# Rows of maxima inside the scores' operands, and maxima set out by a table, in the two 14-wide layers of a four-layer vision network

## What is computed

```python
q, k, v = (xw @ qkv_w + qkv_b) split into 12 heads of 16
attn = q * 16 ** -0.5 @ k.T
attn = attn + rel_h[..., :, None] + rel_w[..., None, :]   # products of q with two small tables
attn = softmax(attn)            # the largest score of each query is subtracted before exp
out = attn @ v                  # then a projection, a residual sum, a norm and an MLP
```

## Time and profile before

| what | value |
|---|---|
| time, median of 3 runs | 605.55 us (603.67 to 606.29) |
| the profiled execution | 607.03 us, of which its span 605.2 us |
| busy, share of the span | PE 88%, PE weight loads 63%, DVE 49%, ACT 38%, POOL 23% |
| mean granted TensorE clock | 0.952 of 2.4 GHz |

### The profile page before, as it was taken

One profiled execution on the slowest core, in us unless ns is written; L12 is line 12 of the kernel. 1 busy time (PEld: TensorE's weight loads), 2 busy tenths in 40 slices (PEclk: granted clock), 3 DMA queues, 4 the chain that ended last, 5 costly groups with the idle time before them and its releaser, 6 DMA issues.

```text
span 605.2 us, 10070 instructions
## 1 busy us (share of the span) xinstructions
PE 530.5 (88%) x3840; PEld 382.5 (63%) x3840; DVE 296.9 (49%) x776; ACT 229.4 (38%) x453; POOL 139.7 (23%) x206
## 2 busy tenths in 40 slices
PE   6968889899988958878888999979879897999997
PEld 4726768674764545455666694756467675848676
DVE  4735866563143552655757452136566755711142
ACT  4304544535335116254544405333235446250210
POOL 8003000103005055073472216020030101120030
PEclk9979998899998979999989999989989898999999
DMA  6893547003312635616637205502916420020001
GB/s 169 190 196 72 118 103 254 1 3 96 94 58 59 134 96 134 155 47 145 145 89 173 114 1 127 123 20 57 192 43 144 92 92 2 2 67 0 1 0 53
DMA packets 21863, 55.39 MB, mean 92 GB/s; under 512 B 4560, under 2 KB 10248, under 8 KB 21688
## 3 DMA queue, kind: packets, MB, share of 16 engines
q1 hardware_dynamic: 21432, 54.65, 37.4%
q0 software_dynamic: 384, 0.10, 0.1%
HBM read 12.28 MB, written 0.79 MB: 22 GB/s over the span
## 4 chain that ended last, share of the span: by engine, by line
PE 62%; DVE 16%; SPq 8%; ACT 5%; DMA 5%; issue 4%; DVEq 0%; ACTq 0%
PE PS L1267 59%; DVE NM L1163 5%; DVE REL L1148 3%; DMA QA<-REL 2%; PE PS L1283 2%; SPq L745 2%; SPq L737 2%; ACT REL L992 2%; SPq L755 1%; DMA PT<-in_qm 1%; SPq L693 1%; ACT OT L953 1%; ACT KD L953 1%; DVE OT L1195 1%; DVE HL L1173 1%
## 5 line engine op out<-in xcount | busy, mean ns | idle before, releaser
L1163 DVE TENSOR_REDUCE NM<-PS 98x2 f32<-98x392 f32 (+2 forms) x192 | 105.7, 569 | 87.4 <-PE PS L1267 86.1
L1012 ACT ACTIVATE PT<-PS 98x392 f32<-98x392 f32 (+2 forms) x192 | 95.5, 518 | 79.0 <-PE PS L1267 77.7
L1267 PE MATMUL PS<-KA,QA 128*98 128x196 f32 (+3 forms) x432 | 90.9, 306 | 27.7 <-DVE NM L1163 22.5
L1267 PE MATMUL PS<-QA,KA 128*98 128x196 f32 (+2 forms) x480 | 91.9, 295 | 10.5 <-ACT PT L1012 5.7
L1267 PEld LDWEIGHTS PS<-KA,QA 128*98 128x98 f32 (+3 forms) x432 | 65.0, 189 | 54.6 <-DVE NM L1163 30.1
L1267 PEld LDWEIGHTS PS<-QA,KA 128*98 128x98 f32 (+2 forms) x480 | 72.9, 191 | 22.6 <-issue 12.4
L1267 PE MATMUL PS<-NR,SEL 128*98 128x392 f32 x144 | 54.4, 378 | 0.6 <-DVE NR L1185 0.6
L1267 PE MATMUL PS<-XT,WQKV 128*128 128x512 f32 (+3 forms) x104 | 49.0, 734 | 6.4 <-issue 3.3
L1267 PE MATMUL PS<-XT,W 128*128 128x512 f32 (+1 forms) x144 | 51.6, 614 | 0.0
L1267 PEld LDWEIGHTS PS<-W,HT 128*128 128x128 f32 x288 | 46.6, 190 | 4.5 <-ACT HT L1033 2.3
L1148 DVE TENSOR_TENSOR REL<-PS,REL 32x512 fp32r<-32x512 f32 (+5 forms) x64 | 28.5, 480 | 42.7 <-ACT REL L992 42.3
(11 more groups left out here) (108 smaller groups left out, 703.0 us busy)
## 6 DMA issues: line engine op xcount, KB each, us to landing
QA<-QHL SPq DMA_DIRECT2D x36, 192.0 KB
KA<-KHL SPq DMA_DIRECT2D x24, 228.0 KB
QA<-REL SPq DMA_DIRECT2D x24, 224.0 KB
QA<-QHL SPq DMA_DIRECT2D x12, 384.0 KB
KA<-KHL SPq DMA_DIRECT2D x12, 384.0 KB
KA<-PT SPq DMA_DIRECT2D x12, 380.0 KB
QA<-REL SPq DMA_DIRECT2D x24, 128.0 KB
W<-in_w SPq DMA_DIRECT2D x3, 768.0 KB, 4.4
```

The lines of the kernel that those rows point to most:

```text
L1012: nc.scalar.activation(dst, src, ACT.Exp).then_inc(probs_done.sem, 1)
L1163: nc.vector.tensor_reduce(dst, src, AX.X, ALU.max, negate=True).then_inc(max_done.sem, 1)
L1267: return nc.tensor.matmul(dst, lhsT, rhs, start=start, stop=stop, skip_group_check=loose)
```

## The change

In the 14-wide layers the maxima become ten rows of the scores' operand. KA has ten constant rows (for each part, high and low, and each of four images and the edges: one where the key belongs to it); QA has ten rows that are zero while the maxima are taken, and hold the negated maxima when the scores are. So the third matmul of each group goes, with `SEL`, `HOT` and the load of `HOT`. The ten rows are filled by another way: the transposed maxima are copied to `NR` by ACT and not by DVE, and then POOL copies them into QA, once in 784 and once in 240 columns. `scores` of a head waits for that (`rows_placed`). Slots of heads 6 to 11 hold an earlier head's maxima, so POOL zeroes the ten rows in the step `aug`, after the earlier head's scores, and the first `max` of the head waits for it (`rows_zeroed`). All other rows move to other places of the slot, with the same DMAs.

Second, the maxima are set out by a table: `add` keeps a running time of PE and DVE by fixed prices in us, and `fill` puts further `max` steps after each step while the reduction before last is finished by that account, up to three heads ahead. Third, the low parts of the second chunk's relative positions become steps of their own (`low`), two steps later, and the split of its k on POOL stands after the fourth maximum of the loop.

```diff
+        if self.pads:
+            self.max_parts = 2 * (NB + 1)
+            self.mask_row, self.rel_row = self.max_parts, 24
+            self.qk_row = self.rel_row + 2 * parts * window
...
+    for part in range(2):
+        for b in range(NB + 1):
+            masks[part * (NB + 1) + b, inner_keys(b) if b < NB else slice(FIRST_EDGE, n)] = 1
...
+PE_SHARE = {"scores": 0.20, "max": 0.18, "maxT": 0.22, "pv": 0.65, "q": 1.4, "k": 1.4, "rh": 0.5, "rw": 0.9}
+DVE_SHARE = {"max": 0.58, "parts": 0.44, "split": 2.6, "rh": 0.6, "rw": 0.6, "inverse": 1.75}
...
+    def add(step):
+        nonlocal now, busy_until
+        out.append(step)
+        if step[0] == "max":
+            now = max(now, reduced[-2])
+        now += PE_SHARE.get(step[0], 0.0)
+        busy_until = max(busy_until, now) + DVE_SHARE.get(step[0], 0.0)
+        if step[0] == "max":
+            reduced.append(busy_until)
+            if step[2] == L.max_units - 1:
+                busy_until += DVE_SHARE["parts"]
...
+    def fill(h, k):
+        needed = L.max_units * (h - 1) + 6 + k
+        while taken < len(maxima) and (taken < needed or
+                                       reduced[-2] <= now and maxima[taken][1] <= h + 3):
+            next_maximum()
...
+            elif step == "aug" and L.pads and i >= L.ring:
+                pool.wait_ge(*scores_psum.at(n, L.units * (i - L.ring + 1) - 1))
+                nc.gpsimd.memset(m["QA"][0:L.max_parts, 0, i % L.ring, :].bitcast(F32), 0.0)\
+                    .then_inc(rows_zeroed.sem, 1)
+            elif step == "maxT" and L.pads:
+                rows, src = m["QA"][0:L.max_parts, 0, i % L.ring, :], m["NR"][:, i % 2, :].bitcast(F32)
+                inner = src.rearrange("r (p q) -> r p q", p=2)[:, :, 0:HALF_IN]
+                pool.wait_ge(*maxT_done.at(n, i))
+                nc.gpsimd.tensor_copy(rows[:, 0:FIRST_EDGE].rearrange("r (b p q) -> r b p q", b=NB, p=2),
+                                      inner.unsqueeze(1).broadcast_to([L.max_parts, NB, 2, HALF_IN]))
+                nc.gpsimd.tensor_copy(rows[:, FIRST_EDGE:], src).then_inc(rows_placed.sem, 1)
...
+            elif step == "maxT" and L.pads:
+                act.wait_ge(*maxT_psum.at(n, i))
+                if i >= 2:
+                    act.wait_ge(*rows_placed.at(n, i - 2))
+                nc.scalar.activation(m["NR"][:, i % 2, :], PS[0:L.max_parts, TR_BANK, 0:2 * L.max_rows],
+                                     ACT.Copy).then_inc(maxT_done.sem, 1)
...
+                    if L.pads and h >= L.ring:
+                        pe.wait_ge(*rows_zeroed.at(n, h - L.ring))
...
-                if k == 0 and not L.pads:
-                    pe.wait_ge(*max_row_at(L, h))
+                if k == 0:
+                    pe.wait_ge(*(rows_placed.at(n, h) if L.pads else max_row_at(L, h)))
...
-                    rows = m["NR"][:, h % 2, :]
...
-                    last = mm(PS[0:size, bank, 0:wide], SEL[:, min(k, NB)].unsqueeze(1).broadcast_to([128, size]),
-                              rows, False, True, True)
```

More of the change, by code:

```diff
@@ L275, in windowed_attention, with next_maximum @@
     maxima = [("max", m, k, 0) for m in range(ahead, HEADS) for k in range(L.max_units)]
-    taken, turned, late = 0, ahead - 1, []
+    taken, turned, now, busy_until = 0, ahead - 1, 0.0, 0.0
+    reduced = [0.0, 0.0]
+    def add(step):
[9 more added lines that the diff above has]
+                busy_until += DVE_SHARE["parts"]
+    def next_maximum():
+        nonlocal taken, turned
+        add(maxima[taken])
+        taken += 1
+        if taken == 4:
+            out.append(("split", 1, 1, 0))
+        while turned < HEADS and turned < ahead + (taken - 2) // L.max_units:
+            add(("maxT", turned, 0, 0))
+            turned += 1
+    def fill(h, k):
[3 more added lines that the diff above has]
+            next_maximum()
     for h in range(HEADS):
@@ L279, in windowed_attention @@
         values = [("pv", first, k, 0) for k in range(L.pv_steps)] if h and h % L.pv_heads == 0 else []
-        goal = min(len(maxima), h * L.max_units + 5)
-        share = goal - taken
+        late = []
+        if h and (h - 1) % L.per_group == 0 and h > L.per_group:
+            g = h // L.per_group - 1
+            late = [(1, ("inverse", g, 0, 0)), (3, ("inverse", g, 1, 0)), (5, ("divide", g, 0, 0))]
+        if taken == len(maxima) and turned < HEADS:
+            add(("maxT", turned, 0, 0))
+            turned += 1
         for k in range(L.units):
-            out.append(("scores", h, k, 0))
+            add(("scores", h, k, 0))
             if h < 2 and k in (1, 4):
                 j = 4 + 2 * h + k // 4
-                out.append((*later[j], O_BANK[j % 2]))
+                add((*later[j], O_BANK[j % 2]))
+            if h < 2 and k in (3, 5):
+                j = 4 + 2 * h + k // 5
+                add(("low", later[j][0], later[j][2], O_BANK[j % 2]))
             if (h, k) == (1, 0):
-                out.append(("split", 1, 0, 0))
+                add(("split", 1, 0, 0))
             if h == 2 and k in (1, 3):
-                out.append(("aug", L.ring + k // 2, 0, 0))
+                add(("aug", L.ring + k // 2, 0, 0))
             if h >= 2 and k == L.units - 1 and h + L.ring < HEADS:
[L293 to L303, removed]
+                add(("aug", h + L.ring, 0, 0))
+            for step in values[k:k + 1] if k < NB else values[NB:] if k == NB else []:
+                add(step)
+                fill(h, k)
+            for at, step in late:
+                if at == k:
+                    add(step)
+            fill(h, k)
+            if taken == len(maxima) and turned < HEADS and k == 2:
+                add(("maxT", turned, 0, 0))
                 turned += 1
@@ L825, in _ @@
         prepare(LAYERS[0])
[L826 to L827 removed]
         for L, step, i, u, bank in all_steps():
             n, m = L.index, mem[L.index]
[L830 removed]
+            if step in ("q", "k") and u == 1 and not L.pads or step == "split" and u and i:
+                if step == "split":
+                    step = "k"
                 half, done, hi_done, lo_done = (m["QHL"], q_done, q_hi, q_lo) if step == "q" else \
@@ L1108, in _ @@
                                         None, ALU.mult).then_inc(skb_done.sem, 1)
+            elif step == "split" and u and i:
+                continue
             elif step == "split" and u:
@@ L1175, in _ @@
                     nc.vector.tensor_tensor(lo, nm, hi.bitcast(F32), ALU.subtract).then_inc(max_lo.sem, 1)
-            elif step == "maxT":
+            elif step == "maxT" and not L.pads:
                 h = i
```

91 lines of the change are left out of this document (36 added, 55 removed).

## The result

| | kernel before | changed kernel |
|---|---|---|
| median of 20 runs each, us | 608.07 (597.53 to 614.84) | 599.18 (596.78 to 604.22) |
| ratio | 1 | 0.9927 (95% interval 0.9901 to 0.9953) |
| profiled execution, span, us | 605.2 | 595.5 |
| mean granted clock | 0.952 | 0.939 |

The ratio leaves out the slowest runs, of which the kernel before has many, so it stands nearer to 1 than the medians (0.985). The change is faster, but by some 4 to 9 us instead of the forecast 23, and 599.18 lies outside the range of 572 to 598.

The account below looks back on a forecast made before the run. The prediction took PE and DVE to bound layers 0 and 2 alternately. Its stretches sum to 11.4 us saved a layer, 22.8 in both, from 607.0 or 605.55 us, giving 583 us; range 572 to 598.

Parts of the forecast that it names:

- What bounds the kernel: Layers 0 and 2, attention: bounds alternate; DVE starves while PE multiplies values, then PE waits for DVE.
- The new wait: Before a head's first scores: chain of 2.65 us through transpose, ACT and POOL, pacing heads without values at 3.8 us.
- Heads 5 to 7: Stretch 84.4 to 101.0: fourteen reductions instead of eighteen, 3.3 us saved a layer (1.2 to 5.9).
- the first stretch: Heads 0 to 2, to head 3's last reduction: 3.9 us saved a layer (0.8 to 6.8), leaving 2.9 for waits.
- The last stretch: Heads 9 to 11, to the last norm: 3.4 us saved a layer (0.5 to 5.6).
- the term for the clock: Heads 9 to 11, to the last norm: 0.6 us added for a low clock.
- Heads with values: Heads 4 and 8: six adding matmuls off (1.1 us), four max steps on (0.7), 0.4 us saved each.
- the fourth rival: Table fails: ten max steps make PE wait, 0.3 us per added one, in heads with values; 588 to 590 us; chance 0.06.
- a sign that the prediction is wrong: Clock rows showing more than some 10 us a layer at 0.50.
- the third rival: Clock falls and stays low in heads without values; a microsecond there loses up to half; 614 us; chance 0.08.

Follow-up runs that it names:

- run 3: The changed kernel with the maxima spread evenly over a head's scores, as in the kernel before: 1.0033 of the kernel before, 607.4 us.
- run 7: The changed kernel with POOL writing each head's ten rows twice: 1.0273 of the kernel before, 617.4 us.
- run 10: The changed kernel with the maxima's parts made by reductions and the second chunk's q split behind head 3's second maximum: 0.9766 of the kernel before, 590.8 us.
- run 6: The changed kernel plus 16 unread products on PE while it waits for head 11's maxima: 0.9899 of the kernel before, 597.1 us.
- run 4: The changed kernel with one maximum after each value step in heads with values: 0.9891 of the kernel before, 600.3 us.
- runs 9: The changed kernel measured again, unedited: 0.9920 of the kernel before, 599.1 us.

## Why the prediction was wrong

- **What bounds the kernel** was right. Matmuls taken from PE give their price where PE is the bound (1.05 us in a head with values, forecast 1.1) and nothing in the whole time (run 3); where the reductions stand decides.
- **The new wait** was right in size and place. From head 3's last reduction (65.73 + 0.47 = 66.20) to its scores (68.78) the changed kernel takes 2.58 us, forecast 2.65. Timeline of that path:

```profile
65.73 0.47 DVE L1238 TENSOR_REDUCE NM<-PS 120x1 f32<-120x312 f32 x1
...
67.14 0.36 ACT L1080 ACTIVATE NR<-PS 10x240 fp32r<-10x240 f32 x1 [0.40 <-PE PS L1466]
...
67.57 0.83 POOL L925 CAST QA<-NR 10x784 fp32r<-10x784 f32 x1 [7.95 <-ACT NR L1080]
...
68.35 0.38 POOL L927 CAST QA<-NR 10x240 fp32r<-10x240 f32 x1
...
68.78 0.25 PEld L1338 LDWEIGHTS PS<-QA,KA 128*98 128x98 f32 x2 [0.31 <-POOL QA L927]
```

  ACT's 0.36 and POOL's 0.83 and 0.38 stand against 0.38, 0.83 and 0.36. Heads 2, 3 and 7 take 3.9 to 4.2 us, forecast 3.8 (head 6, behind a held cast, 6.1), and run 7 shows that the path paces them.
- **Heads 5 to 7** gained 2.85 and 2.7, forecast 3.3, although one cast there is held for 1.43 us.
- **The step that failed** is in the first stretch: "DVE can't take the first low part before 53.2 ... I leave 2.9 us for waits that remain", with the sentence that the split of k on POOL "keeps its place in time", and "the trace shows no stretching so far". POOL's split did keep its place. What the sum put at nothing is DVE standing still beside POOL, and DVE's work had moved there: the maxima of head 2, run ahead, end under POOL's subtraction, their cast is held, and q's split, which then follows without a reduction between, makes PE wait 3.64 us. The casts made by reductions and the split moved (run 10) took 10.6 us off the loops, of the 13.9 that were missing: 6.4 of it in the first stretch, where 5.9 were missing, and 2.9 in heads 5 to 7. Part of this may be the clock, which falls during such a wait; but in layer 0 run 10's loop is 4.7 us shorter with a lower mean clock (0.83 against 0.86), so there the gain isn't the clock's. In layer 2, where it rose from 0.84 to 0.93, the two aren't separated. And I had looked for POOL's instructions to stretch in layers 0 and 2; it was DVE's that did, in layer 1 (379 ns for the smaller cast), and I hadn't read that row.
- **The last stretch**, 3.4 forecast, gave 1.4 and 1.6. Here the term for the clock was too small: the sum had 0.6, and the lower level costs 2.4 and 2.2 us from head 10's scores on (run 6), which is 3.4 of the 3.8 missing. It follows PE's wait of 3.14 us before the transpose, part of which is the cast held behind POOL's division (0.90 us). Head 10's scores start 7.05 us into the stretch, forecast 6.7.
- **Heads with values**: 0.4 saved forecast, 0.15 to 0.45 lost. The four further maxima were put at 0.7 us and cost 0.9 (run 4) to 1.25 (run 3), so the fourth rival's price of 0.3 each was the better one; but the heads behind return it, and the table does what it says.
- **The clock.** In layer 0's loop the mean granted clock fell from 0.93 over 77.9 us to 0.86 over 75.0; with only 1.00 and 0.50 granted, that is 11 us at the lower level (2 x 0.07 x 77.9) and now 21, where more than some 10 was named as a sign that the prediction is wrong. In layer 2's it fell from 0.91 to 0.84. PE fell to the lower level during a wait: the clock is 1.00 from 105.0 to 110.2 and 0.50 from 110.2 to 113.6, while PE stands still for 3.14 us before 111.82. So the third rival's mechanism is there. Where the runs price it (run 6), some 8.3 us at the lower level (2 x 0.46 x 9.19 and 2 x 0.45 x 9.02) cost 2.3, against the half that the rival took.

## What to carry to other kernels

When an order changes, list which instructions of the two engines now run at the same moment, and look all over the trace, other layers included, for a group whose mean is far above that of a like one: it shows what a collision costs. A step taken out of one engine is worth what the next wait leaves of it; here parts made by reductions and one step moved were worth about as much as the change itself (8.3 us between runs 9 and 10).

## What was not expected of the hardware

A DVE cast of ten columns lasted 1.90 us because POOL was subtracting, and a DVE subtraction of two operands on chip 7.02 us instead of 1.53, while reductions beside the same POOL instructions kept their 0.16 to 0.47 us. Sixteen useless products on PE, with which the granted clock stayed at 1.00, made the work behind them 2.2 to 2.4 us shorter (6.79 us instead of 9.19 and 9.02). And the time of layer 1, whose code no edit touches, was 228.0 to 233.7 us in the profiled executions of the changed kernel and its variants, a difference as large as most edits here are worth.
